# A state-space scan kernel: chunk loops written out, the preparation moved earlier, the order of the replication transfers changed

## What is computed

```python
xz = jnp.einsum('bld,ed->ble', seq, in_proj_w)
u, z = jnp.split(xz, 2, axis=-1)
u = silu(sum((up[:, k:k + L, :] * conv_w[:, k] for k in range(D_CONV))) + conv_b)
dt, Bm, Cm = jnp.split(jnp.einsum('bld,ed->ble', u, x_proj_w), [DT_RANK, DT_RANK + D_STATE], axis=-1)
dt = jax.nn.softplus(jnp.einsum('blr,dr->bld', dt, dt_proj_w) + dt_proj_b)
A = -jnp.exp(A_log)
def step(h, inputs):
    dA = jnp.exp(dt_t[:, :, None] * A)
    h = dA * h + (dt_t * u_t)[:, :, None] * B_t[:, None, :]
    return (h, jnp.einsum('bdn,bn->bd', h, C_t))
y = (ys.transpose(1, 0, 2) + u * D) * jax.nn.silu(z)
return jnp.einsum('bld,ed->ble', y, out_proj_w)
```

## Time and profile before

| | |
|---|---|
| median of 3 executions | 1939.89 us (1939.37 to 1941.07) |
| the profiled execution | 1938.45 us |
| its span on the core | 1936.7 us |
| busy in the span | PE 1546.9 us, DVE 1271.6, POOL 1211.5, ACT 991.2 |
| replication transfers, both kinds | 168 + 168, 462.0 KB each |

### The profile page before, as it was taken

One profiled execution on the slowest core, in us unless ns is written; L12 is line 12 of the kernel. 1 busy time (PEld: TensorE's weight loads), 2 busy tenths in 40 slices (PEclk: granted clock), 3 DMA queues, 4 the chain that ended last, 5 costly groups with the idle time before them and its releaser, 6 DMA issues. The chain is left out here.

```text
span 1936.7 us, 25492 instructions
## 1 busy us (share of the span) xinstructions
PE 1546.9 (80%) x6220; PEld 927.2 (48%) x6221; DVE 1271.6 (66%) x2146; ACT 991.2 (51%) x1594; POOL 1211.5 (63%) x1179
## 2 busy tenths in 40 slices
PE   5677777777778998999982687777777777699996
PEld 3222222222228998989981222222222227566664
DVE  5799999999996531111115799999999996411012
ACT  4777777777772211222223777777777772122112
POOL 2699999999981001444435699999999992123310
PEclk8799999999995899999995799999999995599997
DMA  5788777787774204777765877788877881423313
GB/s 131 191 183 185 181 179 177 176 186 179 178 160 155 85 25 143 233 220 218 226 162 134 206 179 176 179 182 179 181 176 174 184 186 49 171 78 122 123 62 107
DMA packets 104507, 311.06 MB, mean 161 GB/s; under 512 B 19389, under 2 KB 74509, under 8 KB 93069
## 3 DMA queue, kind: packets, MB, share of 16 engines
q1 hardware_dynamic: 91896, 291.72, 60.1%
q0 software_dynamic: 12544, 18.63, 4.1%
HBM read 258.83 MB, written 51.45 MB: 160 GB/s over the span
## 5 line engine op out<-in xcount | busy, mean ns | idle before, releaser
L689 POOL TENSOR_TENSOR mamba_dbu<-mamba_rep 128x462 f32<-128x462 f32 x640 | 677.2, 1085 | 66.1 <-DMA mamba_rep<-dt_rows 66.1
L509 PE MATMUL mamba_ysum<-mamba_hc,all_sel 128*128 128x462 f32 x800 | 379.4, 588 | 148.3 <-DVE mamba_hc L797 147.3
L621 ACT ACTIVATE mamba_state<-mamba_rep,all_m_acol 128x462 f32<-128x462 f32 x640 | 388.9, 638 | 156.6 <-DVE mamba_last L808 155.6
L811 DVE TENSOR_TENSOR_SCAN mamba_state<-mamba_state,mamba_carry,mamba_dbu 128x462 f32<-128x462 f32 x400 | 455.4, 1179 | 0.0
L509 PEld LDWEIGHTS mamba_ysum<-mamba_hc,all_sel 128*128 128x128 f32 x800 | 130.3, 190 | 398.3 <-DVE mamba_hc L797 318.8
L808 DVE TENSOR_TENSOR_SCAN mamba_last<-mamba_state,mamba_last,mamba_dbu 128x462 f32<-128x462 f32 x240 | 280.3, 1168 | 15.2 <-POOL mamba_dbu L689 12.4
L684 POOL TENSOR_TENSOR mamba_hcp<-mamba_last,mamba_rep 128x462 f32<-128x462 f32 x240 | 266.7, 1111 | 5.6 <-DVE mamba_last L808 5.6
L504 PE MATMUL mamba_ysum<-mamba_hcp,all_sel 128*128 128x462 f32 x480 | 227.8, 570 | 50.1 <-POOL mamba_hcp L684 50.0
L797 DVE TENSOR_TENSOR mamba_hc<-mamba_state,mamba_rep 128x462 f32<-128x462 f32 (+1 forms) x240 | 230.7, 961 | 0.0
L1433 DVE TENSOR_TENSOR moe_h<-moe_sg,moe_up 128x512 f32<-128x512 f32 x62 | 42.6, 688 | 283.0 <-PE moe_up L1242 276.6
L504 PEld LDWEIGHTS mamba_ysum<-mamba_hcp,all_sel 128*128 128x128 f32 x480 | 85.3, 190 | 172.4 <-POOL mamba_hcp L684 119.6
(11 more groups left out here) (236 smaller groups left out, 2285.6 us busy)
## 6 DMA issues: line engine op xcount, KB each, us to landing
mamba_rep<-bc_rows SPq DMA_DIRECT2D x168, 462.0 KB, 7.4
mamba_rep<-dt_rows SPq DMA_DIRECT2D x168, 462.0 KB, 7.5
weights_wgu<-in_L_gu_dram SPq DMA_DIRECT2D x88, 512.0 KB
dt_rows<-mamba_dd SPq DMA_DIRECT2D x168, 115.5 KB, 7.2
weights_w<-in_L_w_dram SPq DMA_DIRECT2D x16, 1024.0 KB
mamba_xs<-seq_scratch SPq DMA_DIRECT2D x92, 116.0 KB, 9.2
seq_scratch<-mamba_y SPq DMA_DIRECT2D x40, 116.2 KB, 7.0
normed_rows<-xn SPq DMA_DIRECT2D x16, 288.0 KB, 7.1
```

What stands on the lines that cost most here:

```text
L509: nc.tensor.matmul(ysum[:, 0:TC], sel[:, i // NM, :], hc[:, n % HCD, :], start=False, stop=end).then_inc(hc_summed, 1)
L621: nc.scalar.activation(state[:, STATE_BANK[i], 0:TC], rep[:, par * REP_ROWS + i // NM, :], ACT.Exp, scale=m["acol"][:, i:i + 1]).then_inc( ...
L689: pool.tensor_tensor(dbu[:, i % 4, :], rep[:, first + NG + i // NM, :], rep[:, first + 2 * NG + i % NM, :], ALU.mult).then_inc(dbu_ready, 1)
L811: nc.vector.tensor_tensor_scan(bank, bank, dbu[:, i % 4, :], carry[:, i:i + 1], ALU.mult, ALU.add).then_inc(scan_done, 1)
```

## The change

All loops over chunks are written out, so k is a plain number everywhere and the register arithmetic disappears. Within a chunk, the steps of the preparation move:

- PE: `prep_u` and `prep_z` for chunk k + 3 now stand in chunk k after the 11th sum (before: those of k + 2 at the start of chunk k); `prep_dt` and `prep_bc` for k + 2 stand at the start of chunk k (before: after the 4th and 5th sum).
- ACT: silu after item 2 (before 6), exp after 6 (10), one after 7 (11), B and C after 8 (13), ln after 10 (15).
- DVE: the gate after item 3 (2), the rr step after 9 (13), the ln step after 11 and the last addition after 12 (before: both behind item 15).
- POOL: the product dt * u for chunk k + 1 after item 1 (before 3).
- SP: in turn k first `store_dt(k + 1)`; then, when chunk k - 1's step rows have been used, `replicate_dt(k + 1)`; then, when its readouts are done, `replicate_bc(k + 1)`; then `store_bc(k + 2)` and `load_xs(k + 4)`. `dt_rows` has two halves instead of one. `load_xs(3)` stands ahead of the loop.

```diff
-AT_SILU, AT_EXP, AT_ONE, AT_LN, AT_BC, AT_DT, AT_DTU, AT_Y, AT_RR = 6, 10, 11, 15, 13, 3, 3, 2, 13
+AT_SILU, AT_EXP, AT_ONE, AT_BC, AT_LN, AT_U, AT_DTU, AT_Y, AT_RR, AT_LR, AT_ADD = 2, 6, 7, 8, 10, 10, 1, 3, 9, 11, 12
...
             sp.wait_ge(seq_rest, 16 * RESTS)
+            sp.wait_ge(front_mm, START + MMS * 2 + MM_Z)
+            load_xs(3)
             tiles["room_free"](sp)
-            with sp.Fori(0, NCH) as k:
-                sp.reg_mul(replicas, k, 16 * REPS)
-                sp.reg_add(replicas, replicas, 16 * REPS)
-                replicas_before = sp.snap(replicas)
+            for k in range(NCH):
+                replicas_before = 16 * REPS * (k + 1)
                 items_before = START + ITEMS * k
 
+                store_dt(k + 1)
                 sp.wait_ge(decay_ready, items_before)
                 sp.wait_ge(dbu_ready, items_before)
+                sp.wait_ge(rep_loaded, replicas_before)
+                replicate_dt(k + 1)
                 sp.wait_ge(hc_ready, START + ND * k)
                 sp.wait_ge(hcp_ready, START + NP_ * k)
-                sp.wait_ge(rep_loaded, replicas_before)
                 replicate_bc(k + 1)
-                store_dt(k + 1)
-                replicate_dt(k + 1)
-                sp.wait_ge(front_mm, START + MMS * (k + 2) + MM_Z)
-                load_xs(k + 3)
                 store_bc(k + 2)
+                sp.wait_ge(front_mm, START + MMS * (k + 3) + MM_Z)
+                load_xs(k + 4)
...
-            with pe.Fori(0, NCH) as k:
-                prep_u(k + 2)
-                prep_z(k + 2)
-
+            prep_u(2)
+            prep_z(2)
+            for k in range(NCH):
+                prep_dt(k + 2)
+                prep_bc(k + 2)
                 pe.wait_ge(y_ready, START + k)
...
-                    if at == AT_DT:
-                        prep_dt(k + 2)
-                    if at == AT_DT + 1:
-                        prep_bc(k + 2)
+                    if at == AT_U:
+                        prep_u(k + 3)
+                        prep_z(k + 3)
...
                         if i == AT_RR:
                             prep_rr(k + 2)
+                        if i == AT_LR:
+                            prep_ln(k + 2)
+                        if i == AT_ADD:
+                            prep_dt(k + 2)
                         if i - 1 in ON_DVE and not FIRST[i - 1]:
                             read_out(i - 2 if SECOND[i - 1] else i - 1)
-                    prep_ln(k + 2)
                     read_out(ITEMS - 2 if SECOND[ITEMS - 1] else ITEMS - 1)
-                    prep_dt(k + 2)
```

59 lines of the change are left out of this document (24 added, 35 removed).

## The result

| | before | change |
|---|---|---|
| median | 1939.63 us (4 runs, 1938.45 to 1941.07) | 2032.44 us (4 runs, 2029.78 to 2032.70) |
| profiled execution | 1938.45 us, span 1936.7 | 2032.70 us, span 2031.0 |

The ratio is 1.0475 (95% interval 1.0457 to 1.0493): the change makes the kernel 92.8 us slower. I had forecast 53 us more and a range up to 104 us more.

What follows compares the result with a forecast made beforehand. Before, DVE and, without slack, the transfers bound the kernel; the change's transfer loop of 26.8 us per chunk, against 25.35 and 25.43, over 18 cycles per layer plus ends adds 53 us: 1993 us. Range 1944 to 2044.

Steps and rivals of the forecast that it cites:

- With no slack at all: Kernel before: bound by DVE and equally by the transfers, 50.7 us for two chunks, so any lengthening is paid in full.
- the five terms of the loop: Landing to landing in the change: POOL 3.26, store 3.85, first bytes 0.75, copies 17.8, POOL's start 1.1; 26.76 us per chunk.
- Stalls that cost nothing: DVE's waits ahead of items 2 (0.9 us) and 3 (0.75) lie inside the 26.8 us loop and add nothing.
- ACT's table load leaves the boundary: At a chunk's start, the first scan can start 1.15 us after the landing instead of 2.15.
- `load_xs` and `store_bc` at no cost: SP's small transfers behind the copies move during POOL's next product; without that cover about 1 us per chunk.
- the sign I named: SP's longest wait in the loop would be for the landing of `dt_rows`, about 4 us after the first store's issue.
- the hole: Gap of 6 to 8 us between the 18 us windows with full DMA; under 6 us would show the forecast wrong.
- The later steps, "covered": DVE's later waits for ln and the addition are hidden: decay 11 about 18.3 us after landing, DVE there at 18.7.
- Written-out loops, 0: PE's and SP's loop ends vanish; counted as 0 us, since DVE waits only ahead of the first scan.
- Faster copies: Rival: 8 queued copies hold 237 GB/s, taking 16.0 us; loop 25.0, DVE left as bound, 1928 us; chance 0.09.
- Cancelling: Rival: the store's shorter path (2.1 us) offsets the serial order's loss; loop 25.3 to 25.5, 1936 to 1944 us; chance 0.05.
- Stalls not overlapping: Rival: stalls inside the chunk do not overlap the next landing; 28.9 us per chunk, 2066 us; chance 0.07.

Runs made afterwards that it cites:

- The experiment on the product: The change with POOL's dt * u back behind item 3 instead of item 1: 2105.07 us, ratio 1.0869 to the kernel before.
- the store-ahead version: The change with dt * u for chunk k + 2 made at chunk k's end and stored there, behind load_xs: 1977.57 us, 1.0204 of before.
- the last experiment: The kernel before with loops written out, plus ACT's B and C and ln behind item 12 instead of 13 and 15: 1957.50 us, 1.0100 of before.

## Why the prediction was right, and where it was off

**What bounds.** Right about DVE: none of the twelve other versions was measurably faster than the kernel before, and the best with the new places ends at 1.0014, with the store out of the loop and no wait of DVE over 0.3 us. "With no slack at all" for the transfers was too strong: the written-out loops took the table load and 0.43 us of SP's path out of that loop of 50.7 us, and the time stayed (0.9998). For the change this made no difference, since its loop of 27.7 us is 2.6 longer than DVE's shortest chunk with the new places.

**The mechanism.** Right: the five terms of the loop, with DVE in none of them. The experiment on the product shows that the loop is what sets the time. The terms, forecast and measured (in the cycle from POOL's start at 122.89 to its next at 150.21; in brackets the mean over the turns of both layers):

| term | forecast | measured |
|---|---|---|
| POOL, landing to the store's issue | 3.26 | 3.11 (3.20) |
| store's first issue to replication's issue | 3.85 | 4.27 (4.37) |
| issue to first bytes | 0.75 | 0.6 (130.27 to 130.9) |
| 8 copies | 17.8 | 18.3 |
| last bytes to POOL | 1.1 | 1.0 (149.2 to 150.21) |
| the last three together | 19.65 | 19.9 (20.14) |
| sum | 26.8 | 27.3 (27.7) |

**The two mis-sized terms.** The store: I scaled a lone store of 57.8 KB, 1.83 us, to 1.92 for the last of four; it is 4.37 - 1.93 = 2.44. The trace has 2.3 us from a store's issue to its landing as the median of all 168. The Trainium skill (DMA: Bandwidth & Descriptors, "Anatomy of one DMA — SWDGE (gpsimd) path") has about 2.0 us and bytes over 436 GB/s for a transfer on GpSimd's path; SP's stores are not on it, so this is an estimate borrowed from there: the last store would land 2.0 + 0.27 us after its issue, and the term would be 4.2. This case's trace agrees with it better (4.3) than with my 3.85. The copies: I took the mean rate of one kind alone and let the idle shares at the edges fall away; 8 in one row take 18.3 us, which is the sum of 9.2 and 9.6 less 0.5. From replication to the next store it is 23.34 us in the mean against 22.91 in my terms. Both were inside the bounds that the prediction gave.

**The count.** A layer has 19 distances between gates 0 and 19, and 18 of them are turns of the loop, as I had counted. Over those 18 the change is 41.6 us longer in layer 0 and 41.9 in layer 1, 83.5 where I had 50.8: 2.32 us for each turn instead of 1.41. The first distance I had left at its old length; it is 27.2 and 27.1 us instead of 25.4, 3.5 us together. It is no turn of the loop, since it did not grow when the product was moved back. In both layers the first store stands in SP's list behind `load_xs(3)`, and is issued 3.4 and 3.9 us after its product is done; the 1 us that I had allowed was for this. The ends of the loops bring 1.5 where I had 1.2, and 5.8 lie ahead of, between and behind them, mostly scatter, as said above. Together 83.5 + 3.5 + 1.5 + 5.8 = 94.3.

**Stalls that cost nothing.** Right: waits ahead of items 2 and 3, forecast at 0.9 and 0.75, measured at 0.66 and 0.64, lie inside the loop; taking one away won nothing. **ACT's table load leaves the boundary:** right that the first scan starts earlier, 1.4 us after the landing instead of 2.15 (forecast 1.15; ACT's decay ends the wait). It is not the new place of ln that does it: written-out loops alone take the table load ahead of the landing. In the new order it is worth nothing, since DVE is not in the loop.

**`load_xs` and `store_bc` at no cost:** right within the loop: in all 38 turns `load_xs` is issued before the product is done, at the closest by 0.7 us. But the sign I named was wrong: SP's longest wait in the loop is not that for the store's landing (33.2 us in 19) but that of `load_xs` for PE's projection, from 75 to 600 us:

```profile
SPq L320 <- PE mamba_front L442: 247.9, 19, 15.0
SPq L335 <- POOL mamba_dd L632: 56.1, 19, 4.8
...
SPq L348 <- DMA dt_rows<-mamba_dd: 33.2, 19, 2.8
```

It is harmless there, because what stands behind it, the store, is not ready sooner. The size of the hole was also wrong, and by my own terms: 1.1 + 3.26 + 3.85 + 0.75 is 9.0 us, as measured, and not the "6 to 8" that I named as the sign. I had seen that `load_xs` has to wait for item 12's addition and did not ask what would be queued behind it in an experiment; it then cost the store-ahead version 1.7%.

**The later steps, "covered":** half right. In the change DVE never waits there. With the old order and silu and the product moved back it does, at item 11 behind ln, by 0.17 us, and its shortest chunk is 25.37 us instead of 25.08: my 18.3 against 18.7 was a margin of 0.4 us, less than the sizes were good for.

**Written-out loops, 0:** right, 0.9998, though SP's path did get shorter by them.

**The rivals.** Faster copies: 237 GB/s is a microsecond's rate only; the copies' mean is 208 to 210. Cancelling: no, the loop lost 2.3 us more than it won. Stalls not overlapping: no, the period would be 28.9.

**Open.** With the new places and the old order the median is 0.75% above before, the profiled execution 0.5%; the late landings are seen, but what makes some of them late and others not is not shown. How much of the first store's 3.4 and 3.9 us is `load_xs(3)` is not shown either: with SP's order alone, which has no `load_xs(3)`, that store is issued at 69.20 us instead of 71.01. And no trace of the kernel before was taken on the chip on which the loops were written out.

## What to carry to other kernels

Before reordering an in-order transfer queue, write the loop of waits down as a sum: from a landing through whichever engine works on it, the store, its landing, the copies, back to the landing. An order in which every large transfer stands behind a store that has yet to land turns the store's latency and everything ahead of it into time of each turn, even if each transfer by itself is issued "as soon as possible". And a moved step is worth what the bound of that version makes it worth: the same early product won 4% in one order and had a part in a loss of 2% in the other, so parts of a change should be priced in pairs, not one by one. Last, look at the baseline's own trace before testing a term on it: writing out the loops had already moved the table load that the last experiment was to move.
